# Wide compare and multiply instructions for the one-hot tiles of a graph kernel on Trainium2

## The reference

```
# layer 0, twice (relu between, sigmoid behind)
deg  = segment_sum(ew, dst);  dinv = where(deg > 0, rsqrt(deg), 0)     # loops of weight 1 are added
out  = segment_sum((x @ W)[src] * (dinv[src] * ew * dinv[dst]), dst) + b
x    = layernorm(x + sigmoid(h))
# layer 1, attention over the edges of a destination
z = h @ fc_w.T;  rh = r_h @ fc_r_w.T
e = leaky_relu(z[src] @ aw[0] + z[dst] @ aw[1] + rh @ aw[2])
alpha = softmax of e over the edges of each dst
out = relu(segment_sum(alpha * (z[src] + rh), dst) + z @ loop_w)
x    = layernorm(x + out)
```

## Time and profile before

| | us |
|---|---|
| median of 3 timed runs | 3144.19 (3144.05 to 3148.39) |
| span of the profiled execution, which is its own time | 4158.1 |
| DVE busy in it | 1599.5, 7455 instructions |
| POOL busy in it | 2254.0, 2357 instructions |
| PE busy in it | 1810.8, 10379 instructions |

### The profile page before, as it was taken

One profiled execution on the slowest core, in us unless ns is written; L12 is line 12 of the kernel. 1 busy time (PEld: TensorE's weight loads), 2 busy tenths in 40 slices (PEclk: granted clock), 3 DMA queues, 4 the chain that ended last, 5 costly groups with the idle time before them and its releaser, 6 DMA issues. The chain is left out here.

```text
span 4158.1 us, 32695 instructions
## 1 busy us (share of the span) xinstructions
PE 1810.8 (44%) x10379; PEld 1679.2 (40%) x10379; DVE 1599.5 (38%) x7455; ACT 169.0 (4%) x291; POOL 2254.0 (54%) x2357
## 2 busy tenths in 40 slices
PE   1344544333347211443443446003555655555576
PEld 1234444323337111443333446002555555555576
DVE  3555323345447100244444458314222333233343
ACT  0000000000000000000000001000000000000000
POOL 7434666666660776666666650773555555555500
PEclk9756565655557555555555657555666666666677
DMA  3103323334344121112121110222323323332311
GB/s 105 30 24 85 79 61 93 105 111 119 106 119 122 52 53 40 49 53 52 51 53 50 52 42 12 52 55 67 81 72 81 83 75 80 76 84 75 79 57 36
DMA packets 325061, 287.99 MB, mean 69 GB/s; under 512 B 43178, under 2 KB 284769, under 8 KB 324866
## 3 DMA queue, kind: packets, MB, share of 16 engines
q0 software_dynamic: 75072, 155.50, 15.1%
q1 hardware_dynamic: 236886, 123.92, 10.4%
q10 hardware_dynamic: 12924, 6.41, 0.5%
HBM read 272.66 MB, written 13.40 MB: 69 GB/s over the span
## 5 line engine op out<-in xcount | busy, mean ns | idle before, releaser
L499 PE MATMUL ps<-SR,ring 128*128 128x128 f32 (+16 forms) x5844 | 1319.5, 367 | 1582.7 <-DVE SR L900 707.1
L372 POOL DMA_INDIRECT ring<-x_d,srcC x1404 | 1347.3, 960 | 1114.9 <-issue 402.4
L499 PEld LDWEIGHTS ps<-SR,ring 128*128 128x128 f32 x5844 | 1184.4, 283 | 1634.6 <-issue 1615.1
L372 POOL DMA_INDIRECT ring<-h_d,srcC x782 | 751.6, 961 | 484.3 <-issue 230.4
L900 DVE TENSOR_SCALAR SR<-iota,rankC,ewC 128x128 f32<-128x128 f32 x1404 | 395.4, 354 | 413.0 <-issue 247.3
L502 PE MATMUL ps<-SR 128*128 128x128 f32 (+12 forms) x1948 | 508.5, 348 | 80.2 <-issue 79.6
L502 PEld LDWEIGHTS ps<-SR 128*128 128x128 f32 x1948 | 428.1, 268 | 96.2 <-issue 96.0
L1001 DVE SCALAR_TENSOR_TENSOR U<-iota,rankC,U 128x128 f32<-128x128 f32 x782 | 235.0, 346 | 183.0 <-issue 182.5
L924 DVE SCALAR_TENSOR_TENSOR SR<-SR,v2B 128x128 f32<-128x128 f32 x782 | 183.7, 285 | 90.9 <-issue 90.8
L900 DVE TENSOR_SCALAR SR<-iota,rankC,cols 128x128 f32<-128x128 f32 x782 | 211.1, 346 | 2.0 <-issue 0.2
L372 POOL DMA_INDIRECT ring<-in_x_dram,srcC x160 | 153.2, 958 | 97.0 <-issue 48.2
(11 more groups left out here) (166 smaller groups left out, 1039.3 us busy)
## 6 DMA issues: line engine op xcount, KB each, us to landing
SR<-in_edge_attr_dram SPq DMA_DIRECT2D x194, 512.0 KB
ring<-x_d,srcC POOLq DMA_INDIRECT x1404
ring<-h_d,srcC POOLq DMA_INDIRECT x782
U<-lo_d SPq DMA_DIRECT2D x20, 256.0 KB
x_d<-rows SPq DMA_DIRECT2D x12, 264.0 KB
x_d<-rows SPq DMA_DIRECT2D x7, 448.0 KB, 5.2
rows<-in_x_dram SPq DMA_DIRECT2D x6, 512.0 KB
h_d<-rows ACTq DMA_DIRECT2D x12, 256.0 KB
```

The lines of the kernel that those rows point to most:

```text
L372: pool.indirect_dma_start(ring[:, gg % R, k, 0:width], None, (x if p == 0 and q < R0 else table)[:, :], bass.IndirectOffsetOnAxis(ap=srcC[ ...
L499: last = nc.tensor.matmul(ps[(p * NK + k) % 2][:, lo:hi], ring[:, gg % R, j, 0:D], S[:, gg % NS, j, w0:w0 + hi - lo], start=False, stop=t ...
```

## The change

The eight one-hots of a group are made by one instruction over 1024 columns (8 tiles x 128) instead of eight over 128. For the degree stage this is one `tensor_tensor` that compares the row 0 to 127 (`iota`, repeated for each tile by a stride of zero) with the eight columns of `rankC` (each repeated 128 times). It reads f32 and writes bf16; the bf16 copy `iota_h` is dropped. For the passes it is two, a compare into S and a multiply of S in place with the eight weight columns, with a `link` between them. The eight `tensor_scalar`s before did compare and multiply in one instruction each, with both per-partition values as scalar operands. The last group has 6 tiles. Nothing else changes: the semaphores that others wait for are the same, and so are the buffers.

```diff
@@ the constants
-        iota_h = sb("iota_h", [P, P], BF16)
...
-            v.tensor_copy(iota_h[:, :], iota_i[:, :])
@@ the degree stage
+            def spread(n):
+                return iota[:, :].unsqueeze(1).broadcast_to([P, n, W])
+
+            def rank_of(q, n):
+                return rankC[:, q * GT:q * GT + n].unsqueeze(2).broadcast_to([P, n, W])
+
             for q in range(G):
                 if q >= ND:
                     dve.wait_ge(s("deg_summed"), q - ND + 1)
-                for j, t in enumerate(tiles(q)):
-                    last = v.tensor_scalar(SH[:, q % ND, j, :], iota_h[:, :], rankC[:, t:t + 1], None, ALU.is_equal)
-                last.then_inc(s("deg_onehot"), 1)
+                n = len(tiles(q))
+                v.tensor_tensor(SH[:, q % ND, 0:n, :], spread(n), rank_of(q, n), ALU.is_equal).then_inc(s("deg_onehot"), 1)
@@ build_S, for each group of each pass
                 if gg >= NS:
                     dve.wait_ge(s("summed"), gg - NS + 1)
-                for j, t in enumerate(tiles(q)):
-                    last = v.tensor_scalar(S[:, gg % NS, j, :], iota[:, :], rankC[:, t:t + 1], w[:, t:t + 1], ALU.is_equal, ALU.mult)
-                last.then_inc(s("S_built"), 1)
+                n = len(tiles(q))
+                link(v.tensor_tensor(S[:, gg % NS, 0:n, :], spread(n), rank_of(q, n), ALU.is_equal))
+                v.tensor_tensor(S[:, gg % NS, 0:n, :], S[:, gg % NS, 0:n, :], w[:, q * GT:q * GT + n].unsqueeze(2).broadcast_to([P, n, W]), ALU.mult
+                                ).then_inc(s("S_built"), 1)
```

## The result

| | before | after |
|---|---|---|
| timed, median | 3145.36 us (3144.05 to 3148.39, 4 runs) | 3280.61 us (3277.19 to 3284.47, 4 runs) |
| profiled span | 4158.1 us, again recorded 3141.5 us (below) | 3278.0 us |
| POOL busy | 2254.0 us, again 2282.4 us | 2419.0 us |

A forecast was written before the change was run, and what follows sets the result against it. The timed kernel was taken as a chain of gathers on POOL. Degree stage 48, passes 0 and 1 115, pass 2 27, old delays -15, longer one-hots 5: 180 us on 3144, say 3320 us; 8-in-10 range 3140 to 3460.

The forecast's parts named there:

- The 209 us beside the gathers: Start, pass changes and tail: what the timed 3144 us holds besides 2935 us of gathers and their issue.
- Rival three: POOL doesn't set the timed run; slow issue is partly there, so fewer DVE starts help: about 3000 us, chance 0.07.
- rival two: tensor_tensor doesn't delay gathers at all, in degree stage or passes: about 3115 us, chance 0.11.
- Rival one: A gather is kept out over both wide instructions of a group: about 3660 us, chance 0.11.
- the linked instruction at 18.14: Earlier profile: an instruction after a 0.04 us wait didn't keep a waiting gather out; used against losing the hand-over.
- slack at the store of x1: Degree stage: POOL gets a few us of slack there, so 48 us were counted instead of 51.
- a phase taken as even: Passes: a gather's read falls anywhere in the first wide instruction, mean wait 0.62 us, 0.6 us a group.
- the old delays: Gather waits behind the small one-hots, which go: 294 groups at about 0.05 us, 15 us saved (0 to 40).
- longer one-hots on the path: Pass 2: TensorE waits for 0.37 us longer builds after each of 13 finished banks: 5 us (0 to 15).
- The "balanced" 9.9 us a group: Pass 2: TensorE and DVE take 9.9 us a group against 10.0 us of gathers.
- Rival four: Another engine's chain has more slack against POOL and absorbs most of the delay: 3150 to 3200 us, chance 0.11.
- the likeliest case: The forecast itself, gathers delayed behind wide instructions: about 3320 us, own range 3240 to 3430, chance 0.60.

The follow-up runs named there:

- the earlier trace: The first profile of the kernel before, no edit: span 4158.1 us beside a timed median of about 3145 us.
- the passes alone: Against the kernel before, wide compare and multiply only in the passes, small one-hots in the degree stage: 3233.69 us, ratio 1.0274.
- the PSUM operand: Wide one-hots only in the passes; in passes 0 and 1 one operand in PSUM (except 20 groups' weights), pass 2 as before: 3140.32 us.
- the compare alone: Wide instructions only in the passes, small degree one-hots, with the multiply left out: 3223.17 us, ratio 1.0246 to the kernel before.
- the run with four tiles: Wide instructions only in the passes, each cut in two of 512 columns, both compares, then both multiplies: 3232.45 us, ratio 1.0272.
- the second recording of before: The kernel before, unchanged, profiled once more: timed 3143.35 us, span 3141.5 us.

## Why the prediction was right, and where it was off

- **The bound.** The timed kernel is a chain of gathers: right, and now seen in a recording (37 us of other waits). The 209 us beside the gathers were taken from the slow recording; in the second one the gathers and their issue are 2996 us, and 146 us are left. The reason given for the earlier trace rows was wrong. Recording doesn't slow the issue; one recording was slow, and nothing shows why. With it fell the forecast of a profiled span of about 3900 us; it was 3278.0. Rival three (the slow issue is partly in the timed run) fell by the same recording.
- **The mechanism.** Read 0.12 to 0.18 us into a gather, wait until the DVE instruction with two SBUF inputs ends, end 0.8 us later: right at every row shown, for all 172 gathers of the passes alone, and the PSUM operand excludes the other causes. The Trainium skill, "SBUF — State Buffer", Who interferes with whom, has the rule that two SBUF inputs contend with GpSimd, and this case agrees, with gathers of 1.79 us in the mean beside a multiply that has its weights in SBUF and of 0.94 beside the same one with them in PSUM. Its second statement, that tensor_tensor doesn't hold up a DMA issued there, was rival two (3115 us); for these indirect DMAs 1.97 us beside 0.94 decides against it.
- **Length and pair.** 1.23 us and a second instruction that costs nothing: measured 1.22, 0.04 apart, and free for the gathers by the compare alone. Rival one (a gather kept out over both) would have shown gathers of 2.5 to 3.3 us; the longest of the 2346 takes 2.19. But the ground that the forecast gave against it doesn't hold: the linked instruction at 18.14 in the earlier trace rows is a cast with one input, so it says nothing of a hand-over between two with two inputs. There the forecast was right by luck, and without the link's wait the hand-over is lost in 19 of 76 cases (the run with four tiles).
- **The degree stage.** 48 forecast, 49 measured; a period of 2.28 forecast, 2.27 measured. The delay, put at 51 us, came as 49.6. The few us taken off for slack at the store of x1 don't exist (POOL doesn't wait there), so that 48 and 49 agree so closely is in part luck.
- **The passes, the mis-sized terms.** 0.6 us a group, from a phase taken as even, with the remark that it need not be. With half of the new wait in pass 2 absorbed and the old delays off, that made 53 + 53 + 22 us, and 5 for longer one-hots on the path. The passes alone measured 39 + 12 + 39. Counted gather by gather, the waits behind the compares are 53, 18 and 35 us in the three passes, where an even phase gives 58, 58 and 59. So the even phase was near for pass 0 and far off for pass 1, where 0.13 us a group were left; shifted by 0.6 us, pass 1 costs 0.45. In pass 2 the phase gave less too, but nothing of it was absorbed (window +40 us, gathers +38.9). TensorE wasn't the bound there: in the second recording of before it waits for DVE in pass 2 and never for a gather, and 108 us follow the last gather where the slow recording had 208. The "balanced" 9.9 us a group read from the earlier trace rows belong to that recording, in which the ring was full, and include the tail. Rival four (another chain absorbs) fell with it. The old delays of the small one-hots were 0.03 us a group in pass 1 against 0.05.

So the time came out at 3281 for 3320, inside the likeliest case's own range, for the reason given, and with two errors that partly cancel: passes 0 and 1 were put 54 us too high and pass 2 12 us too low.

## What to carry to other kernels

Where GpSimd issues indirect gathers back to back, each DVE instruction that reads two SBUF operands can hold one up by the rest of its length, and sometimes by the next such instruction as well where no wait parts them; before instructions are merged, count the gathers beside them, and where the merge is wanted put one operand in PSUM. The price of such a wait is not length times chance: the phase is set by what releases the instruction, so read it from a timeline or bound it from both sides. Where the profiled span and the timed median differ by a third, record again before anything is built on the difference.

## What the runs showed of the hardware that was not expected

- One recording of the kernel before was 1.32 times as long as the next of the same kernel (4158.1 and 3141.5 us), with DVE starting in steps of 1.41 us beside the gathers; the changed kernel and the eight other edits had spans within 0.3% of their timed medians.
- Halving the wide instructions left the time where it was (3232.45 against 3233.69 us), since 22 us less behind the compares met 21 us more behind the multiplies; moving the pairs by 0.6 us cost 69 us.
- A gather was kept out over two unlinked compares of 0.68 us in 19 of 76 cases, and never over a compare and the multiply linked to it.
- A copy of one 128-column row in PSUM, read there instead of in SBUF, with two other operands moved alike, gave 1.6% (3090.04 us) to a kernel whose time is set by its gathers.
